# Two shifted-window attention layers on one core: statistics by pairs of images, two-part output projection, a separate order for the last images, and unread products on TensorE

## The chip, the cores and the metric

The kernel runs on one core of one Trainium2 chip. The metric is the device time of the whole program in microseconds (us); lower is better. The kernel before ran twice, at 763.71 and 770.17 us, so its median is 766.94 us. A further, profiled execution took 770.32 us.

## The reference, cut to what matters

The input is 32 images of 16 x 16 tokens with 256 channels, in float32. The same block is applied twice, each time with its own weights:

```
x = x + attention_0(group_norm(x))
x = x + attention_1(group_norm(x))

group_norm(v): 32 groups of 8 channels; mean and variance over the 256 tokens and the 8 channels
attention(x):
    xs = roll(x, (-4, -4)), cut into 4 windows of 8 x 8 = 64 tokens
    q, k = xw @ Wq.T, xw @ Wk.T;  v = xw @ Wv.T + bv       16 heads of 16 channels
    qn, kn = q / max(|q|, 1e-12), k / max(|k|, 1e-12)
    logits = qn @ kn.T * exp(min(logit_scale, log 100)) + 16 * sigmoid(bias table) (-inf across the shift's seams)
    o = softmax(logits) @ v
    z = o @ Wo.T + bo, windows put back, roll(z, (4, 4))
```

The bias table comes from a small two-layer network over 225 relative positions and is the same for all images of a layer. Nothing links one image to another, but an image's second layer needs its first.

## The kernel before, in words

**Jobs and rounds.** A job is one image in one layer; there are 64 (32 images, then the same 32 in layer 1). All x stays on the chip as `x_all`, with channels on the partitions. The work is a hand-written software pipeline. In round j every engine runs its `iteration(j, ...)`, which touches four jobs: `now` = j, `before` = j-1, `older` = j-2, `oldest` = j-3. Ahead of them come the group statistics of job j+3 (WARM = 3), the group roots of job j+2 and the normalised input of job j+1. Rounds -3 to 66 are run (`run`, L211 to L225). Most are bodies of hardware loops of two rounds each, in which semaphore counts and image addresses are computed in registers: on TensorE rounds 4 to 61, on the other engines rounds 4 to 27 and 36 to 59 (SyncE's first loop ends at 25). The rest are written out with constants. No scheduler moves anything: each engine runs its instructions in the written order, and semaphores alone tie the engines together.

**What TensorE does in a round** (`iteration`, L512 to L537): `sum_groups` of job j+2 (L433, one product that averages the statistics over groups); `project_qk` of `now` (L380, two halves of six products of 512 columns, into the two banks of `ps_qk`); `turn_back` of `oldest` (L392, four transposes of the attention output into `ps_mix`); `turn` of `before` (L404, eight transposes of q and k); `project_out` of `oldest` (L414 and L419: eight products with the rounded part `mixed_hi`, then four with the rest, into the same bank `z_cols` of `ps_mix`, with one signal `z_done` after all twelve); `score` of `before` (L469, 32 row-tiled products of 32 rows by 64 columns); `mix` of `older` (L486, one product of 64 rows and 128 columns, then L496, 63 products of 64 x 64, into `ps_mix`); `project_v` of `now` (L508, twelve products, into the second bank of `ps_qk`). An fp32 product is two instructions in the trace, so 32 products are 64 there.

**What waits for what.** `mix` overwrites the bank that `project_out` filled, so its first product (L486) waits until VectorE has added both halves of the residual (`add_residual`, L794, signal `x_updated`); that waits for `z_done`. `project_v` waits for `unit_ready`: ScalarE squares q and k (L574), VectorE sums (L758), ScalarE takes a logarithm and an exponential as seed (L609, L618), GpSimd does a Newton step (L943 to L953), VectorE scales (L783). ScalarE turns scores into `probs` by `exp`, in two instructions of 1024 columns (L643); GpSimd multiplies them by `exp_bias` in four (L963). VectorE divides (`divide`, L816 to L823) after `mix` and so gives `o_rows` to `turn_back` one round later.

**Start and end.** Layer 0's `exp_bias` is made from the bias table, which goes out to memory and comes back spread over the partitions (`keep_table`, `spread_bias`); four VectorE multiplications (L737) in round 0 finish it. SyncE issues x loads six jobs ahead, each when the last but one has landed. After round 63 the rounds simply run on with ever fewer jobs; all of them use the same `ps_mix`, so each `mix` waits for the residual before it. A flag, computed from the least softmax sum, decides at the end whether the whole is repeated in a slower exact form; on this input it is not.

## Time and profile before

| | us |
|---|---|
| two runs | 770.17, 763.71 (median 766.94) |
| profiled execution | 770.32 |
| its span, first to last instruction | 768.5 |
| TensorE busy | 728.5 (95%) |
| GpSimd busy | 553.6 (72%) |
| VectorE busy | 503.5 (66%) |
| ScalarE busy | 498.5 (65%) |

The span is the time from the first to the last instruction of the one profiled execution; 1.8 us of its 770.32 lie around it. A busy TensorE is not TensorE at its peak: matmuls are pipelined, and the end of one is modelled. "PEld" is its weight load, which overlaps the products. A gap of TensorE is read best from the end of a weight load to the start of the next. Its clock is granted at one of two levels, 2.4 GHz (shown as 1.00) or 1.2 GHz (0.50); a window in between has both.

### The profile page before, as it was taken

The numbers are of one execution on the slowest core, as the hardware profiler recorded it, in microseconds if no ns is written. First come the engines' busy times: TensorE is split into PE (matmuls) and PEld (weight loads), VectorE is DVE, ScalarE is ACT, GpSimd is POOL, SyncE is SP. The second block draws the span as 40 slices with busy tenths as digits, with TensorE's granted clock in tenths as the row PEclk, the third lists the DMA queues.
The fourth block names the chain that finished last, engine by engine and source line by source line (L and its number), as shares of the span: only waits on it lengthen the run. The fifth ranks groups of instructions, "written<-read, shape, count | busy, mean of one in ns | idle before, by whom it ended". The sixth has DMA issues, their size and how long they took to land.

```text
span 768.5 us, 38488 instructions
## 1 busy us (share of the span) xinstructions
PE 728.5 (95%) x15518; PEld 652.5 (85%) x15518; DVE 503.5 (66%) x1177; ACT 498.5 (65%) x848; POOL 553.6 (72%) x913
## 2 busy tenths in 40 slices
PE   3689899999999999999999999999999999999995
PEld 3578788888888889898989888888888888888984
DVE  4545466666666666667777667677766767776642
ACT  4556467676677667676777676666667666666650
POOL 4475668777877787788888777877777787777660
PEclk9789899999999999999999999999999999999995
DMA  4666200000000000000000000000000000000000
GB/s 116 156 157 172 65 0 0 0 1 0 0 0 0 0 0 0 0 0 0 1 0 0 28 28 14 27 27 25 16 27 27 14 27 27 27 14 27 29 31 32
DMA packets 14041, 21.45 MB, mean 28 GB/s; under 512 B 3756, under 2 KB 5045, under 8 KB 14005
## 3 DMA queue, kind: packets, MB, share of 16 engines
q1 hardware_dynamic: 13461, 20.23, 8.8%
q10 hardware_dynamic: 544, 0.79, 0.3%
q8 instruction: 17, 0.28, 0.2%
q14 instruction: 19, 0.16, 0.1%
HBM read 12.60 MB, written 8.42 MB: 27 GB/s over the span
## 4 chain that ended last, share of the span: by engine, by line
PE 89%; issue 3%; DVE 3%; DMA 2%; DVEq 1%; ACT 0%; SPq 0%; ACTq 0%
PE ps_qk L380 24%; PE ps_mix L496 17%; PE ps_qk L508 14%; PE ps_mix L414 9%; PE ps_score L404 7%; PE ps_score L469 6%; PE ps_mix L419 4%; PE ps_mix L392 4%; PE ps_mix L486 3%; DVE x_out L794 2%; DMA bias_rev<-table_scratch 1%; PE ps_score L433 1%; DMA table_scratch<-table 1%; DMA cpb<-in_L_cpb 0%; DVE exp_bias L737 0%
## 5 line engine op out<-in xcount | busy, mean ns | idle before, releaser
L963 POOL TENSOR_TENSOR probs<-probs,exp_bias 128x512 f32<-128x512 f32 x256 | 326.0, 1305 | 18.9 <-ACT probs L643 18.9
L380 PE MATMUL ps_qk<-w_qk,xn 128*128 128x512 f32 x768 | 200.0, 410 | 0.0
L643 ACT ACTIVATE probs<-ps_score,lower 128x1024 f32<-128x1024 f32 x128 | 135.7, 1111 | 66.8 <-PE ps_score L469 66.8
L380 PEld LDWEIGHTS ps_qk<-w_qk,xn 128*128 128x128 f32 x768 | 144.0, 194 | 30.2
L496 PE MATMUL ps_mix<-v_ones,probs 64*64 64x17 f32 x8064 | 133.4, 209 | 3.4 <-issue 3.4
L574 ACT ACTIVATE squares<-ps_qk 128x512 f32<-128x512 f32 x128 | 77.0, 602 | 87.1 <-PE ps_qk L380 87.1
L758 DVE TENSOR_REDUCE sums_sq<-squares 128x32 f32<-128x512 f32 x128 | 87.2, 682 | 68.9 <-ACT squares L574 68.8
L496 PEld LDWEIGHTS ps_mix<-v_ones,probs 64*64 64x64 f32 x8064 | 126.8, 136 | 5.5 <-issue 3.7
L783 DVE SCALAR_TENSOR_TENSOR unit<-root,ps_qk 128x512 f32<-128x512 f32 x128 | 82.4, 683 | 58.9 <-POOL root L953 58.9
L508 PE MATMUL ps_qk<-w_v,xn 128*128 128x256 f32 x768 | 113.9, 300 | 5.4 <-DVE unit L783 4.6
L508 PEld LDWEIGHTS ps_qk<-w_v,xn 128*128 128x128 f32 x768 | 100.2, 198 | 7.7 <-issue 6.0
L943 POOL TENSOR_TENSOR refined<-sums_sq,seed 128x66 f32<-128x66 f32 (+2 forms) x66 | 21.3, 322 | 97.6 <-ACT seed L618 97.5
L651 ACT ACTIVATE v_ones<-ps_qk 128x512 f32<-128x512 f32 x64 | 38.4, 601 | 77.4 <-PE ps_qk L508 77.4
L919 POOL TENSOR_TENSOR xn<-xn 128x512 fp32r<-128x512 f32 x64 | 82.0, 1281 | 5.5 <-ACT xn L581 5.5
L596 ACT ACTIVATE q_own<-ps_score,own_head 128x512 f32<-128x512 f32 x128 | 81.1, 693 | 0.0
L414 PE MATMUL ps_mix<-mixed,w_o 128*128 128x256 f32 x512 | 78.5, 296 | 1.4 <-ACT mixed L588 1.4
L469 PE MATMUL ps_score<-q_own,k_rows 32*64 32x128 f32 x4096 | 77.2, 278 | 2.4 <-DVE k_rows L767 1.2
L414 PEld LDWEIGHTS ps_mix<-mixed,w_o 128*128 128x128 f32 x512 | 65.0, 190 | 9.1 <-ACT mixed L588 2.0
L626 ACT ACTIVATE xn<-x_all,g_off,root 128x256 f32 (+1 forms) x128 | 69.5, 596 | 3.3 <-POOL g_off L956 3.3
L469 PEld LDWEIGHTS ps_score<-q_own,k_rows 32*64 32x64 f32 x4096 | 61.8, 130 | 11.2 <-ACT q_own L596 2.8
L404 PE MATMUL ps_score<-ident,unit 128*128 128x128 f32 x512 | 66.3, 273 | 0.0
L404 PEld LDWEIGHTS ps_score<-ident,unit 128*128 128x128 f32 x512 | 58.0, 140 | 0.3
(73 smaller groups left out, 867.8 us busy)
## 6 DMA issues: line engine op xcount, KB each, us to landing
x_all<-in_x SPq DMA_DIRECT2D x32, 256.0 KB, 3.1
out<-x_out SPq DMA_DIRECT2D x32, 256.0 KB, 2.1
bias_rev<-table_scratch SPq DMA_DIRECT2D x4, 452.0 KB
w_qk_in<-in_L_matrices ACTq DMA_DIRECT2D x1, 512.0 KB, 4.6
w_o_in<-in_L_matrices SPq DMA_DIRECT2D x4, 128.0 KB
w_qk_in<-in_L_matrices SPq DMA_DIRECT2D x1, 512.0 KB, 5.5
w_v_in<-in_L_matrices ACTq DMA_DIRECT2D x1, 256.0 KB, 4.9
w_v_in<-in_L_matrices SPq DMA_DIRECT2D x1, 256.0 KB, 6.2
```

The costliest lines, as they stand in the source:

```text
L380: last = nc.tensor.matmul(ps_qk[:, e, :], xn[:, px, t.parity, c, e * P:(e + 1) * P], w_qk[:, pw, c, :], start=(c == 0 and i == 0), stop=(c ...
L404: last = nc.tensor.transpose(to[:, e, c, :], unit[:, e, (n * CC + c) * P:(n * CC + c + 1) * P], ident[:, :])
L414: nc.tensor.matmul(z_cols[:, c, :], w_o[:, part, a, c * P:(c + 1) * P], mixed[:, 0, a, :], start=(c + a + part == 0), stop=False, skip_gro ...
L469: last = nc.tensor.matmul(ps_score[w * N:(w + 1) * N, r, cols:cols + 2 * N], k_rows[at, e, c, w * N:(w + 1) * N], q_own[at, e, c, w, :, :] ...
L496: last = nc.tensor.matmul(mix_cols[a * N:(a + 1) * N, w, (e * CC + c) * GROUPS + r, :], probs[at, t.parity, r, e, c, a, :], v_ones[at, t.p ...
L508: last = nc.tensor.matmul(v_cols[:, e, :], xn[:, px, t.parity, c, e * P:(e + 1) * P], w_v[:, pw, c, :], start=(c == 0 and i == 0), stop=(c ...
L596: nc.scalar.activation(q_own[:, :, :, :, a, :].rearrange("p e c w n -> p (e c w) n"), q_turned_to.rearrange("p e c (w n) -> p (e c w) n", ...
L643: nc.scalar.activation(probs[:, t.parity, 2 * i:2 * i + 2, :, :, :, :].rearrange("p r e c a n -> p r (e c a n)"), ps_score[:, 2 * i:2 * i ...
L758: nc.vector.tensor_reduce(sums_sq[:, e * NORMS:(e + 1) * NORMS], squares[:, e, :].rearrange("p (h d) -> p h d", d=HD), AX_X, ALU.add).then ...
L783: nc.vector.scalar_tensor_tensor(out=unit[:, e, :].rearrange("p (h d) -> p h d", d=HD), in0=by, scalar=INV_NORM_TOP, in1=ps_qk[:, e, :].re ...
L919: nc.gpsimd.tensor_tensor(xn[:, 1, t.parity, :, :], xn32[:, :, :], xn[:, 0, t.parity, :, :], ALU.subtract).then_inc(xn_ready, 1)
L963: nc.gpsimd.tensor_tensor(pr, pr, exp_bias[:, t.layer, r, :, :, :, :].rearrange("p e c a n -> p (e c a n)"), ALU.mult).then_inc(weighted, 1)
```

## The change

It rewrites the rounds, the start and the end together.

- **Statistics by pairs.** `sum_groups`, `group_variance` and the group part of the root chain run in even rounds only, for jobs j+2 and j+3 together (four columns instead of two). The moments are taken four jobs ahead (AHEAD = 4). The last variance step gets a tensor of fours in place of a constant.
- **TensorE's round.** `turn_back` of `oldest` goes between the halves of `project_qk`. `project_out` finishes channel half 0 (four products with the rounded part, two with the rest), signals, then half 1, and signals again. `mix` begins with one tiny product of 32 rows, 64 columns and one output column that carries its waits, and then has all 64 products in 64 x 64 form; its waits for `v_ready` and `mixed_ready` are gone.
- **The others' rounds.** ScalarE rounds `mixed` ahead of `xn` and takes `exp` in four instructions of 512 columns. VectorE forms `mixed`'s rest between the two sums of squares, and each half of the residual waits for its own signal.
- **Start.** Both first images are loaded first; the bias tables of the two layers are made apart (layer 1's in rounds 0 and 1); layer 0's `exp_bias` is multiplied by GpSimd in round 1; the sum of output biases moves from round 1 to 2; TensorE gets unread products (`keep_busy`: 7, 3, 9 and 12). SyncE holds the x loads from round 4 on until `unit_ready` has counted six jobs.
- **End.** After round 63 a `drain` of its own follows. The last three jobs use three different places for `mix`, `turn_back` and `project_out`: `ps_mix`, `ps_qk` and `ps_score`. The last job's weighting is shared between GpSimd and VectorE, its `mix` is split in halves around `turn_back` of the job before, and its output is stored in two halves. Three unread products stand ahead of the last `turn_back` and five behind it. Eight tiny memsets on GpSimd (into `unread`) stand in round 60.

```
+AHEAD = 4
...
-        def both_passes(engine, iteration, loops=((4, 28), (IMAGES + 4, 60))):
+            half, parity = divmod(JOBS - 1 + JOBS * exact, 2)
+            drain(Job(half, parity, None, exact))
...
+        def pair(j, base):
+            return job(j, base, 2) if j % 2 == 0 else None
+        def home_of(t, last):
+            return (ps_mix, ps_qk, ps_score)[last]
+        def back_of(t, last):
+            return home_of(t, last)[:, 1, :].rearrange("p (a t) -> p a t", a=2)
+        def kept_of(t, last):
+            return xn[:, :, 0, :, :] if last == 2 else mixed
...
SyncE
+                if j == 4 and not base.exact:
+                    sp.wait_ge(unit_ready, 2 * 6)
                 if j >= 0:
                     load_x(job(j, base, PREFETCH))
...
TensorE, project_out
+                for c in range(CC):
                     for a in range(2):
                         for part in range(2):
-                                             start=(c + a + part == 0), stop=False, skip_group_check=True)
-                pe.wait_ge(mixed_ready, t.count(1, 1))
-                for c in range(CC):
+                            nc.tensor.matmul(home[:, c, 0:TOKENS], w_o[:, part, a, c * P:(c + 1) * P], kept[:, 0, a, :],
+                                             start=(a + part == 0), stop=False, skip_group_check=True)
+                    if c == 0:
+                        pe.wait_ge(mixed_ready, t.count(1, 1))
                     for a in range(2):
+                        done = nc.tensor.matmul(home[:, c, 0:TOKENS], w_o[:, 0, a, c * P:(c + 1) * P], kept[:, 1, a, :],
                                                 start=False, stop=(a == 1), skip_group_check=True)
-                last.then_inc(z_done, 1)
+                    done.then_inc(z_done, 1)
TensorE, mix
-                past(pe, x_updated, t.count(2, 0))
-                past(pe, mixed_ready, t.count(1, 0))
-                pe.wait_ge(v_ready, t.count(1, 1))
-                pe.wait_ge(weighted, t.count(4, 4))
-                nc.tensor.matmul(mix_cols[:, 0, 0, :], probs[0:N, t.parity, 0, 0, 0, :, :]...
+                if last == 0:
+                    past(pe, x_updated, t.count(2, 0))
+                    pe.wait_ge(weighted, t.count(4, 4 - 2 * t.exact))
+                    nc.tensor.matmul(ps_mix[0:N, 0, 511:512], ident[0:32, 0:N], ident[0:32, 0:1], start=True, stop=True, skip_group_check=True)
...
TensorE, iteration
+                if j != 0:
+                    sum_groups(j, base)
+                if j == -1 and not base.exact:
+                    keep_busy(9)
                 project_qk(now, 0)
+                turn_back(oldest)
                 project_qk(now, 1)
-                turn_back(oldest)
+                if j == 0:
+                    sum_groups(j, base)
+                    if not base.exact:
+                        begin_table(1)
+                        keep_busy(12)
+                        end_table(1)
                 turn(before)
                 project_out(oldest)
+                if j == 2 and not base.exact:
+                    sum_out_bias()
-                score(j, base, before)
+                score(before)
...
+            def drain(base):
+                now, before, older = (job(JOBS - 1, base, -k) for k in range(3))
+                turn(now)
+                turn_back(older)
+                score(now)
+                project_out(older)
+                mix(before, 1)
+                mix(now, 2, (0,))
+                turn_back(before, 1)
+                mix(now, 2, (1,))
+                project_out(before, 1)
+                if not base.exact:
+                    keep_busy(3)
+                turn_back(now, 2)
+                if not base.exact:
+                    sum_lost()
+                    keep_busy(5)
+                project_out(now, 2)
+            def keep_busy(n):
+                ones = v_ones[:, 0, :, :, :, :, :].rearrange("p e c r a d -> p (e c r a d)")[:, 0:P]
+                for _ in range(n):
+                    nc.tensor.matmul(ps_score[:, 3, 0:P], ones, ones, start=True, stop=True, skip_group_check=True)
...
ScalarE, iteration
                 square(now, 0)
+                keep_mixed(oldest)
                 round_xn(job(j, base, 1))
                 square(now, 1)
-                keep_mixed(oldest)
...
-                for i in range(GROUPS // 2):
-                    exp(before, i)
+                for r in range(GROUPS):
+                    exp(before, r)
...
VectorE, add_residual and drain
+                dve.wait_ge(z_done, t.count(2, c + 1))
...
+                keep_k(now)
+                keep_rest(older)
+                for r in (1, 3):
+                    dve.wait_ge(exped, now.count(4, r + 1))
+                    multiply_probs(nc.vector, now, r, last_weighted)
+                divide(before, 1)
+                for c in range(CC):
+                    add_residual(older, c)
+                keep_rest(before, 1)
+                divide(now, 2)
...
+                for c in range(CC):
+                    add_residual(before, c, 1)
+                keep_rest(now, 2)
...
+                for c in range(CC):
+                    add_residual(now, c, 2)
...
GpSimd, iteration
+                if j == 1 and not base.exact:
+                    for e in range(2):
+                        for c in range(CC):
+                            multiply_bias(nc.gpsimd, 0, e, c)
...
+                if j == JOBS - 4:
+                    for k in range(8):
+                        nc.gpsimd.memset(unread[:, k:k + 1], 0.0).then_inc(moment_step, 1)
```

TensorE, round 3 (the first round with every step, written out), before:

```order
L433 MATMUL ps_score<-bn_sum,consts 128x4
L380 MATMUL ps_qk<-w_qk,xn 128x512 x12
L392 MATMUL ps_mix<-ident,o_rows 128x2x64 x4
L404 MATMUL ps_score<-ident,unit 128x128 x8
L414 MATMUL ps_mix<-mixed,w_o 128x256 x8
L419 MATMUL ps_mix<-mixed,w_o 128x256 x4
L469 MATMUL ps_score<-q_own,k_rows 64x128 x32
L486 MATMUL ps_mix<-v_ones,probs 128x17
L496 MATMUL ps_mix<-v_ones,probs 64x17 x63
L508 MATMUL ps_qk<-w_v,xn 128x256 x12
```

The same round in the changed kernel:

```order
L450 MATMUL ps_qk<-w_qk,xn 128x512 x6
L463 MATMUL ps_mix<-ident,o_rows 128x2x64 x4
L450 MATMUL ps_qk<-w_qk,xn 128x512 x6
L475 MATMUL ps_score<-ident,unit 128x128 x8
L487 MATMUL ps_mix<-mixed,w_o 128x256 x4
L492 MATMUL ps_mix<-mixed,w_o 128x256 x2
L487 MATMUL ps_mix<-mixed,w_o 128x256 x4
L492 MATMUL ps_mix<-mixed,w_o 128x256 x2
L544 MATMUL ps_score<-q_own,k_rows 64x128 x32
L561 MATMUL ps_mix<-ident 64x1
L577 MATMUL ps_mix<-v_ones,probs 64x17 x64
L590 MATMUL ps_qk<-w_v,xn 128x256 x12
```

The group product is gone from this odd round, the transposes stand inside the projection, the first channel half of the output is signalled six products earlier, and the 128-column product at the head of `mix` has become one of 64 columns by one.

TensorE, the end of the program, before (from the last `score` on):

```order
L469 MATMUL ps_score<-q_own,k_rows 64x128 x32
L486 MATMUL ps_mix<-v_ones,probs 128x17
L496 MATMUL ps_mix<-v_ones,probs 64x17 x63
L392 MATMUL ps_mix<-ident,o_rows 128x2x64 x4
L414 MATMUL ps_mix<-mixed,w_o 128x256 x8
L419 MATMUL ps_mix<-mixed,w_o 128x256 x4
L486 MATMUL ps_mix<-v_ones,probs 128x17
L496 MATMUL ps_mix<-v_ones,probs 64x17 x63
L541 MATMUL ps_score<-consts,lost 1x1
L392 MATMUL ps_mix<-ident,o_rows 128x2x64 x4
L414 MATMUL ps_mix<-mixed,w_o 128x256 x8
L419 MATMUL ps_mix<-mixed,w_o 128x256 x4
```

And now, from the `mix` of the last job but one:

```order
L577 MATMUL ps_qk<-v_ones,probs 64x17 x64
L577 MATMUL ps_score<-v_ones,probs 64x17 x32
L463 MATMUL ps_qk<-ident,o_rows 128x2x64 x4
L577 MATMUL ps_score<-v_ones,probs 64x17 x32
L487 MATMUL ps_qk<-mixed,w_o 128x256 x4
L492 MATMUL ps_qk<-mixed,w_o 128x256 x2
L487 MATMUL ps_qk<-mixed,w_o 128x256 x4
L492 MATMUL ps_qk<-mixed,w_o 128x256 x2
L656 MATMUL ps_score<-v_ones 128x128 x3
L463 MATMUL ps_score<-ident,o_rows 128x2x64 x4
L660 MATMUL ps_mix<-consts,lost 1x1
L656 MATMUL ps_score<-v_ones 128x128 x5
```

The last two jobs' `mix` stand next to each other, in other banks; the last job's twelve output products follow behind the rows shown.

GpSimd in round 1 of the changed kernel:

```order
L1085 TENSOR_TENSOR xn<-xn 128x512
L1109 TENSOR_TENSOR refined<-sums_sq,seed 128x64
L1111 TENSOR_TENSOR refined<-refined,seed 128x64
L1113 TENSOR_TENSOR refined<-threes,refined 128x64
L1119 TENSOR_TENSOR root<-refined,seed 128x64
L276 TENSOR_TENSOR exp_bias<-bias_rev,masks 128x4x128 x4
L282 TENSOR_TENSOR probs<-probs,exp_bias 128x512 x4
```

The row L276 is new here: the four bias products stood on VectorE in round 0 before (L737).

## Rows read from the trace of the kernel before

**Rows 1.** The page: engines' busy time, granted clock in 40 slices, chain of waits.

```profile
PE 728.5 (95%) x15518; PEld 652.5 (85%) x15518; DVE 503.5 (66%) x1177; ACT 498.5 (65%) x848; POOL 553.6 (72%) x913
...
PEclk9789899999999999999999999999999999999995
```

**Rows 2.** Stretches: start:end, length, busy of PE, PEld, DVE, ACT, POOL; PEclk, DMA, GB/s.

```profile
107.98:729.73 621.75, 615.69 (x13548) 552.61 (x13549) 433.42 (x1007) 429.93 (x729) 479.70 (x775) 1.00 0.03 12
...
704.28:715.20 10.92, 10.92 (x243) 9.87 (x242) 6.78 (x16) 7.65 (x13) 7.74 (x11) 1.00 0.06 24
715.20:725.90 10.70, 10.70 (x245) 9.65 (x240) 6.00 (x12) 7.64 (x13) 7.82 (x11) 1.00 0.07 25
...
749.60:768.50 18.90, 10.46 (x158) 9.28 (x158) 4.80 (x13) 0.60 (x2) 1.19 (x1) 0.53 0.09 33
```

**Rows 3.** Groups by line, 107.98 to 729.73 us: busy, mean ns | idle before.

```profile
L486 PEld LDWEIGHTS ps_mix<-v_ones,probs 64*128 64x128 f32 x112 | 16.5, 185 | 18.9 <-issue 18.7 <-DVE x_out L794 0.2
```

**Rows 4.** Timeline of a layer-1 round in the loops: start, length, engine, line, idle before.

```profile
512.19 0.63 PE L419 MATMUL ps_mix<-mixed,w_o 128*128 128x256 f32 x4
...
512.75 0.96 PEld L469 LDWEIGHTS ps_score<-q_own,k_rows 32*64 32x64 f32 x64
512.75 1.21 PE L469 MATMUL ps_score<-q_own,k_rows 32*64 32x128 f32 x64
...
513.09 0.88 DVE L794 SCALAR_TENSOR_TENSOR x_out<-ps_mix,out_bias,x_all 128x256 f32<-128x256 f32 x2 [0.57 <-PE ps_mix L419]
...
514.09 0.29 PEld L486 LDWEIGHTS ps_mix<-v_ones,probs 64*128 64x128 f32 x2 [0.37 <-issue]
...
514.41 1.95 PEld L496 LDWEIGHTS ps_mix<-v_ones,probs 64*64 64x64 f32 x126
514.75 1.28 DVE L783 SCALAR_TENSOR_TENSOR unit<-root,ps_qk 128x512 f32<-128x512 f32 x2 [0.79 <-POOL root L953]
...
516.39 1.48 PEld L508 LDWEIGHTS ps_qk<-w_v,xn 128*128 128x128 f32 x12
...
517.13 0.69 DVE L823 TENSOR_TENSOR o_rows<-ps_mix,inv_sums 128x512 f32<-128x512 f32 x1
...
518.05 1.18 PE L380 MATMUL ps_qk<-w_qk,xn 128*128 128x512 f32 x4
```

**Rows 5.** Timeline of round 63, all engines written out, no group product.

```profile
735.47 0.96 PEld L469 LDWEIGHTS ps_score<-q_own,k_rows 32*64 32x64 f32 x64
735.47 1.21 PE L469 MATMUL ps_score<-q_own,k_rows 32*64 32x128 f32 x64
735.58 0.88 DVE L794 SCALAR_TENSOR_TENSOR x_out<-ps_mix,out_bias,x_all 128x256 f32<-128x256 f32 x2 [0.34 <-PE ps_mix L419]
...
736.60 0.29 PEld L486 LDWEIGHTS ps_mix<-v_ones,probs 64*128 64x128 f32 x2 [0.17 <-DVE x_out L794]
```

**Rows 6.** Timeline of the start.

```profile
12.17 1.29 POOL L919 TENSOR_TENSOR xn<-xn 128x512 fp32r<-128x512 f32 x1 [1.78 <-ACT xn L581]
...
16.94 4.53 PE L380 MATMUL ps_qk<-w_qk,xn 128*128 128x512 f32 x12
...
27.56 3.98 DVE L737 TENSOR_TENSOR exp_bias<-bias_rev,masks 128x512 f32<-128x512 f32 x4 [1.05 <-DMA bias_rev<-table_scratch]
...
37.33 4.98 POOL L963 TENSOR_TENSOR probs<-probs,exp_bias 128x512 f32<-128x512 f32 x4 [0.29 <-ACT probs L643]
...
78.73 2.63 PEld L508 LDWEIGHTS ps_qk<-w_v,xn 128*128 128x128 f32 x12
```

**Rows 7.** Timeline of the end, after round 63.

```profile
740.43 0.62 PE L392 MATMUL ps_mix<-ident,o_rows 128*128 128x128 f32 x4
...
744.85 2.05 PE L496 MATMUL ps_mix<-v_ones,probs 64*64 64x17 f32 x126
...
753.31 3.60 PE L496 MATMUL ps_mix<-v_ones,probs 64*64 64x17 f32 x126
...
763.50 0.88 DVE L794 SCALAR_TENSOR_TENSOR x_out<-ps_mix,out_bias,x_all 128x256 f32<-128x256 f32 x2 [2.30 <-PE ps_mix L419]
```

462 lines of the change are left out of this document (271 added, 191 removed).

## Prediction

> **What bounds the kernel now.** I read the page first. TensorE is busy for 728.5 of 768.5 us, no other engine for more than 553.6 [rows 1], so the kernel is a chain of TensorE work. Next I cut the span by the clock row of the page and by stretches. From round 7's first projection (107.98) to round 63's (729.73), 56 rounds pass in 621.75 us at clock 1.00 [rows 2]: 11.10 us a round. Ahead of that lie 107.98 us for seven rounds and a start, behind it 38.8 us. So there are three places: the steady rounds (81% of the span), the start, the end.
>
> In a steady round TensorE is never idle for long; the groups by line show where it is. Ahead of L486, the first product of `mix`, it stood idle for 18.9 us in these 56 rounds, 0.34 us each [rows 3]. The row says "issue", so I went to the timeline: in layer 1 the loads of `score` end at 513.71, the second residual on VectorE at 513.97, L486 starts at 514.09 [rows 4]. In round 63, where registers need not be computed, they end at 736.43 and 736.46, and L486 starts at 736.60 [rows 5]. The start keeps 0.12 to 0.14 us behind the residual while the gap itself changes from 0.38 to 0.17. The gap is VectorE's residual, and VectorE began it late because `z_done` comes once, after all twelve products, and register work adds 0.27 us to it in the loop (512.82 to 513.09) [rows 4].
>
> **The steady rounds.** Four edits touch TensorE's time.
> 1. Group product every second round. The round from 704.28 has one (10.92 us), the next has none (10.70) [rows 2]. It costs 0.22, so half, 0.11, goes per round. This is sure.
> 2. The gap. Half 0 of the residual now starts when the first six products are done, under the other six and the transposed k; only half 1 is left behind the last product. From 512.82 with the same 0.27 us of register work and half of the 0.88 us it ends at 513.53, before the loads of `score` end at 513.71 [rows 4]. What remains is the change of step. Lower bound: 0.03 us, from the end of L486's loads (514.38) to L496's start (514.41) [rows 4], a change of form without a wait. Upper bound: the 0.17 of round 63 [rows 5]. I take 0.12, nearer the upper end, since two waits stand in this step and none in the other. Against the mean of 0.34 [rows 3] that saves 0.22, between 0.17 and 0.30.
> 3. The first product. L486 takes 514.09 to 514.41, 0.32 us [rows 4]. In its place come a 32 x 64 product with one column (two instructions) and one more 64 x 64 product (two). The 126 instructions of L496 load in 1.95 us, 15.5 ns each, and the 64 of L469 in 0.96, 15 ns each [rows 4]: four of these are 0.06 us. With a change of form (0.04 to 0.07) I take 0.13, so 0.19 saved. Bounds: nothing saved, or 0.26.
> 4. `turn_back` inside the projection and the split `project_out` issue the same instructions; on TensorE I cost them at nothing. Their cover is that `o_rows` is ready at 517.82 and the projection begins at 518.05 [rows 4]; the transposes now come six products (1.4 us) after that, so VectorE may be 1.6 us late before TensorE feels it.
>
> Sum: 0.11 + 0.22 + 0.19 = 0.52 us a round, low 0.28, high 0.67. Over 57 rounds (7 to 63) this is 29.6 us, from 16 to 38. I take 28, because something is late next: `project_v` needs the first unit, ready at 515.39, and starts at 516.39 [rows 4]. That is 1.0 us of slack, of which edits 2 and 3 use 0.4. ScalarE squares the second half later by the transposes (0.62 us in the end's row [rows 7]), but `mixed`, which stood behind these squares, now stands ahead of them, so the logarithm moves by little. Four `exp` in place of two cost ScalarE two more instructions; it is busy 429.93 of 621.75 us [rows 2] and nothing on TensorE waits for the last of them within the round. GpSimd's 479.70 us [rows 2] gain nothing new but the eight memsets, well under 1 us once.
>
> **The start.** Job 0's input is complete on GpSimd at 13.46 (12.17 + 1.29), but the first projection starts at 16.94 [rows 6]: TensorE's group product for job 2 stood ahead of it. It is moved behind, so 3.4 us go. Then 91.0 us pass for rounds 0 to 6, against 7 x 11.10 = 77.7: 13.3 us of waits, half clock and pauses in TensorE's stream. Half clock shows in L508's twelve loads, 2.63 us at 78.73 [rows 6] against 1.48 in the steady round [rows 4]. The 31 unread products of the start and the held x loads work against both, and the sum of output biases leaves the path of round 1. Against this, GpSimd gets four bias products in round 1. No row has them on GpSimd. VectorE took 3.98 us for the four, and GpSimd 4.98 for four contiguous products of the same size [rows 6]; I take 5, and twice that as the upper bound. They stand ahead of job 0's weighting and of round 2's Newton step and I count 4 of the 5 us on the path in round 2. Of the 13.3 us I count 10 as won back, since round 0 waits for its own chain with nothing else to do in either kernel. Balance: 3.4 + 10 - 4 = 9 us gained. Bounds: 3.4 + 0 - 5, so about 2 lost (the whole bias price on the path and none of the 13.3 back), and 3.4 + 13.3 = 17 gained.
>
> **The end.** From 740.43 to the last residual's end (763.50 + 0.88 = 764.38) it takes 23.95 us [rows 7], and three times `mix`, transposes, projection and residual follow each other in one bank, with the clock at 0.53 after 749.6 [rows 2]. L496 then takes 3.60 us instead of 2.05 [rows 7]. I laid the new order out by hand from these lengths at full clock, in us after 740.43: turn 0.9, turn back 1.4, `score` 2.1 to 3.3 (it waits for q on ScalarE), `exp` to 5.7, the first `project_out` to 4.9, `mix` of the last but one to 7.0, GpSimd and VectorE end weighting at 6.6, first half of the last `mix` 8.0, second 9.9, divided 11.8, turned back 12.3, `mixed` 13.1 and its rest 13.9, the projection's halves 14.1 and 14.9, last residual 15.4. That saves 8.5. Half clock in the last projections could give back 1 to 3 us; the unread products (as long as a transpose each, a quarter of the 0.62 us of four [rows 7]) stand where TensorE waits for VectorE anyway. I take 8, from 5 to 10. The last store is of half the size, which I count at nothing.
>
> **Sum.** 28 + 9 + 8 = 45 us. Against the profiled execution's own 770.32 us (span 768.5 and 1.8 around it) that is 725.3. The median of the two runs lies 3.4 us below the profiled execution, so I put the forecast between the two, at **724 us**. All low ends together give 770 - 19 = 751, all high ends 705; together they are unlikely.
>
> **Rivals.**
> - *The change of form rules the gap.* What if L486 waits for the array to empty, as its start 0.13 us after the modelled end of L469's last product (513.96) would allow [rows 4]? Then splitting `z_done` gains nothing, edits 2 and 3 save only what the shorter product does (0.15), and a round gains 0.26: 15 us instead of 28, so **737 us**. Against it: with the same forms the gap is 0.17 in round 63, and L486 starts there before that modelled end (735.47 + 1.21 = 736.68) [rows 5]. Chance 0.08. The Trainium skill, TensorEngine Tiling (Array Packing), Key Properties, says that changing the tiling mode drains TensorE. By that rule the pause stays and the time would be the 737 us above; the trace bounds the pause of a change of form at the 0.17 us of round 63, and so speaks for a small one.
> - *The unit chain becomes the bound.* Later squares and longer ScalarE work use up the 1.0 us of slack, and the round stays at 10.9. Against it: ScalarE's work ahead of the logarithm is the same in sum, and VectorE's too. It gives 56 x 0.2 = 11 us in place of 28: **741 us**. Chance 0.07.
> - *Slower: `turn_back` stalls the projection.* It now stands in front of the second half, whose squares feed the sums, the Newton step, the units, and at last `divide`, which feeds `turn_back`. If `o_rows` comes more than 1.6 us later than in rows 4, each round waits in mid-projection and the delay feeds itself, since VectorE is in order. From 2.1 us late a round is longer than 11.10; at 2.7 us the rounds lose 34 us, and the whole stands at **787 us**. Against it: VectorE is busy 433.42 of 621.75 us [rows 2]. Chance 0.02.
> - *The start fails.* GpSimd's bias products are twice as long as their nearest row and the clock does not hold: the start loses 2 to 5 instead of gaining 9, which gives **737 us**. Chance 0.08, inside the range. On the price, the Trainium skill, GPSIMD Engine Reference, Engine selection, has two-input elementwise work about twice as slow on GpSimd as on VectorE. By that page the four would take twice the 3.98 us of VectorE, an estimate of 8 us, and the time would be some 3 us above my sum.
>
>
> **Chances and range.** Forecast 0.75, the others as above. A measurement of this kernel can tell about 2%, 15 us, from no change: 751.6 us and below is faster. All rivals but the slower one are faster still; I keep 0.05 for within 2% (several low ends at once) and 0.03 for slower, 0.92 for faster. The range that leaves out 2 in 10 reaches from 709 (start and rounds near their high ends) to 740.
>
> **What would show it.** Idle ahead of the first `mix` product near 0.1 us; round time 10.6 us in both layers, with the difference between layers gone; first projection near 13.5 us; no gap ahead of `turn_back` inside the projection; round 7 at some 96 us; the last residual 16 us after the last `project_v`. I would be wrong if `project_v` or the second projection half showed a new wait, if the gap stayed at 0.3 us, or if GpSimd's bias products took over 2 us each.

## The result, and the profile after

The changed kernel takes **713.38 us** (two runs, 713.31 and 713.44) against 766.94 of the kernel before: a ratio of 0.930, with a 95% interval of 0.913 to 0.947. Run again, four times beside seven runs of before (median 769.83), it took 713.49, ratio 0.9263 (0.9217 to 0.9309). The forecast was 724 with a range of 709 to 740. So the sign, the mechanism and the range held; the sum was 11 us short. Its three terms missed by 15 us (the rounds, more gained), 1 us (the start, more) and 5 us (the end, less), so that the end's miss covered a part of the rounds'. One of all executions of the kernel before took 2373.71 us, for a reason that no profile shows, and is left out of the ratios. The profiled execution took 713.44 us, of which 711.6 are the span: 56.9 less than the 768.5 before.

Page of the changed kernel: busy time by engine, the granted clock in 40 slices, the shares of the chain of waits.

```profile
PE 690.4 (97%) x15658; PEld 632.6 (89%) x15658; DVE 468.6 (66%) x1049; ACT 518.6 (73%) x976; POOL 551.2 (77%) x888
...
PEclk8979999999999999999999999999999999999998
...
PE 92%; POOL 3%; DVE 2%; issue 2%; DMA 1%; ACT 1%; SPq 0%; POOLq 0%; DVEq 0%; ACTq 0%
```

Beside [rows 1], TensorE is busy 38 us less in all, and its idle time went from 40 us to 21: some was work that is gone, some was waiting. Where, the stretches tell. First the 56 rounds from round 7's first projection to round 63's, then round 63.

```profile
97.87:677.09 579.22, 578.22 (x13611) 530.57 (x13610) 400.08 (x894) 447.80 (x842) 474.19 (x753) 1.00 0.06 19
677.09:687.35 10.26, 10.26 (x244) 9.44 (x243) 5.94 (x12) 6.46 (x12) 6.42 (x10) 1.00 0.07 26
```

Against [rows 2] the account of the 56.9 us is:

| stretch | before | after | gained | forecast |
|---|---|---|---|---|
| up to round 7 | 107.98 | 97.87 | 10.1 | 9 |
| 56 rounds, 7 to 62 | 621.75 | 579.22 | 42.5 | 27.5 |
| round 63 | 10.70 | 10.26 | 0.4 | 0.5 |
| to the last residual's end | 23.95 | 20.69 | 3.3 | 8 |
| from there to the span's end | 4.12 | 3.56 | 0.6 | 0 |

(The timeline of before has round 7's first product at 107.84, where [rows 2] has 107.98: 0.1 us between the first two rows of the table.)

Of the signs that the prediction named, the round time came out at 10.34 us and not 10.6, and alike in both layers (two rounds took 20.64 us from 97.87 on in layer 0 and 20.61 from 408.90 on in layer 1); the idle time ahead of the first `mix` product is 0 and not 0.1; the first projection started at 15.70 and not near 13.5; round 7 at 97.87 and not 96.

A round fell from 11.10 to 10.34 us, 0.76, where the sum had 0.52 and, rounded down, gave 0.49. The timeline of one round of layer 1, with the group product of the next round at its end (start, length, engine, line; elsewhere brackets say how long the engine had been idle, and for whom; "issue" there is idle time for which the profile shows no wait). One fp32 product is two loads, so the 64 products of `mix` are 128 loads here:

```profile
408.79 1.23 PEld L450 LDWEIGHTS ps_qk<-w_qk,xn 128*128 128x128 f32 x6
...
410.06 0.59 PEld L463 LDWEIGHTS ps_mix<-ident,o_rows 128*128 128x128 f32 x4
...
410.62 1.24 PEld L450 LDWEIGHTS ps_qk<-w_qk,xn 128*128 128x128 f32 x6
...
411.90 1.03 PEld L475 LDWEIGHTS ps_score<-ident,unit 128*128 128x128 f32 x8
...
412.90 0.54 PEld L487 LDWEIGHTS ps_mix<-mixed,w_o 128*128 128x128 f32 x4
...
414.17 1.02 DVE L929 SCALAR_TENSOR_TENSOR x_out<-ps_mix,out_bias,x_all 128x256 f32<-128x256 f32 x2
414.44 0.35 ACT L739 ACTIVATE seed<-logs,consts 128x64 f32<-128x64 f32 x1
414.48 0.96 PEld L544 LDWEIGHTS ps_score<-q_own,k_rows 32*64 32x64 f32 x64
...
415.43 0.19 PEld L561 LDWEIGHTS ps_mix<-ident 32*64 32x64 f32 x2
...
415.63 1.96 PEld L577 LDWEIGHTS ps_mix<-v_ones,probs 64*64 64x64 f32 x128
...
417.61 1.46 PEld L590 LDWEIGHTS ps_qk<-w_v,xn 128*128 128x128 f32 x12
...
419.00 0.30 PEld L508 LDWEIGHTS ps_score<-bn_sum,consts 128*128 128x128 f32 x2
...
419.22 1.25 PEld L450 LDWEIGHTS ps_qk<-w_qk,xn 128*128 128x128 f32 x6
```

Three things to see, each against [rows 4]. The two residuals (L929) end at 415.19, the loads of `score` (L544) at 415.44, and the head of `mix` (L561, its first small product) starts at 415.43: no pause at all, where 0.34 stood in the mean [rows 3]. From the head to the first of the 128 loads it is 0.20 us, where L486 took 0.32. And the twelve products of the projection with the transposes between them take 1.27 + 0.56 + 1.28 = 3.11 us, where the same sixteen instructions took 2.67 + 0.56 = 3.23 in round 62 of before. The group product still costs its 0.22 (419.00 to 419.22), in every second round.

### The profile page after: what moved, and what is told of

Same layout as the page of the kernel before. It is cut to its first block, busy times and chain, and to the rows that moved or that the text cites. A ratio compares the mean times of both kernels' runs of the same rounds, so it can differ in the third digit from the quotient of the medians.

```text
span 711.6 us, 38739 instructions
## 1 busy us (share of the span) xinstructions
PE 690.4 (97%) x15658; PEld 632.6 (89%) x15658; DVE 468.6 (66%) x1049; ACT 518.6 (73%) x976; POOL 551.2 (77%) x888
## 4 chain that ended last, share of the span: by engine, by line
PE 92%; POOL 3%; DVE 2%; issue 2%; DMA 1%; ACT 1%; SPq 0%; POOLq 0%; DVEq 0%; ACTq 0%
PE ps_qk L450 25%; PE ps_mix L577 17%; PE ps_qk L590 14%; PE ps_score L544 9%; PE ps_mix L487 8%; PE ps_score L475 7%; PE ps_mix L492 4%; PE ps_mix L463 4%; PE ps_score L656 1%; POOL probs L282 1%; DMA x_all<-in_x 1%; POOL exp_bias L276 1%; PE ps_score L508 1%; DVE probs L282 0%; PE ps_score L577 0%
## 5 line engine op out<-in xcount | busy, mean ns | idle before, releaser
L450 PE MATMUL ps_qk<-w_qk,xn 128*128 128x512 f32 x768 | 209.4, 409 | 0.2
L764 ACT ACTIVATE probs<-ps_score,lower 128x512 f32<-128x512 f32 x256 | 155.2, 689 | 56.2 <-PE ps_score L544 56.1
L450 PEld LDWEIGHTS ps_qk<-w_qk,xn 128*128 128x128 f32 x768 | 136.6, 191 | 24.3 <-DVE unit L919 0.2
L577 PE MATMUL ps_mix<-v_ones,probs 64*64 64x17 f32 x7936 | 129.1, 208 | 2.0 <-issue 2.0
L577 PEld LDWEIGHTS ps_mix<-v_ones,probs 64*64 64x64 f32 x7936 | 122.7, 136 | 5.1 <-issue 2.2
L590 PE MATMUL ps_qk<-w_v,xn 128*128 128x256 f32 x768 | 109.2, 293 | 5.4 <-DVE unit L919 5.4
L590 PEld LDWEIGHTS ps_qk<-w_v,xn 128*128 128x128 f32 x768 | 96.2, 194 | 7.5 <-DVE unit L919 4.2
L1109 POOL TENSOR_TENSOR refined<-sums_sq,seed 128x64 f32<-128x64 f32 (+1 forms) x65 | 22.0, 338 | 82.1 <-ACT seed L739 82.1
L487 PE MATMUL ps_mix<-mixed,w_o 128*128 128x256 f32 x496 | 82.4, 288 | 0.0
L544 PE MATMUL ps_score<-q_own,k_rows 32*64 32x128 f32 x4096 | 77.2, 278 | 1.6 <-ACT q_own L717 1.5
L544 PEld LDWEIGHTS ps_score<-q_own,k_rows 32*64 32x64 f32 x4096 | 61.7, 130 | 9.8 <-ACT q_own L717 2.0
L487 PEld LDWEIGHTS ps_mix<-mixed,w_o 128*128 128x128 f32 x496 | 66.2, 189 | 0.2 <-issue 0.2
```

What stands on the lines that cost most here:

```text
L450: last = nc.tensor.matmul(ps_qk[:, e, :], xn[:, px, t.parity, c, e * P:(e + 1) * P], w_qk[:, pw, c, :], start=(c == 0 and i == 0), stop=(c ...
L487: nc.tensor.matmul(home[:, c, 0:TOKENS], w_o[:, part, a, c * P:(c + 1) * P], kept[:, 0, a, :], start=(a + part == 0), stop=False, skip_gro ...
L544: last = nc.tensor.matmul(ps_score[w * N:(w + 1) * N, r, cols:cols + 2 * N], k_rows[at, e, c, w * N:(w + 1) * N], q_own[at, e, c, w, :, :] ...
L577: done = nc.tensor.matmul(mix_cols[a * N:(a + 1) * N, w, (e * CC + c) * GROUPS + r, :], probs[at, t.parity, r, e, c, a, :], v_ones[at, t.p ...
L590: last = nc.tensor.matmul(v_cols[:, e, :], xn[:, px, t.parity, c, e * P:(e + 1) * P], w_v[:, pw, c, :], start=(c == 0 and i == 0), stop=(c ...
L764: nc.scalar.activation(probs[:, t.parity, r, :, :, :, :].rearrange("p e c a n -> p (e c a n)"), ps_score[:, r, :], ACT.Exp, bias=lower[:, ...
```

## The experiments

All ran beside the kernel before. The changed kernel itself ran only in the first of three such sets, and the medians of before were 769.83, 769.69 and 770.86 us in them, so a difference of about a microsecond to the changed kernel says nothing. The differences below are between medians (to 713.49 where nothing else is said), and where a stretch is given it is from the profiled execution: round 7's first projection to round 63's, 579.22 us in the changed kernel (579.25 in its second profile) and 621.75 in the kernel before.

**again**: the changed kernel, unedited.

> The changed kernel once more, on the chip and in the job of the three that follow, so that each of them is read against it. Every theory expects the 713 us of its first runs, within 2 us, and some 0.93 of the kernel before.

713.49 us (710.34 to 714.77). Its profile has the same 56 rounds to 0.03 us, while the ends of two profiles of one kernel differ by 1 us. So the rounds can be read to a few hundredths, the start and the end only to about one microsecond.

**one_signal**: the residual waits for both halves again.

```diff
-                dve.wait_ge(z_done, t.count(2, c + 1))
+                dve.wait_ge(z_done, t.count(2, c + 1 if last else 2))
```

> In the rounds both halves of the residual wait for the second signal of the output projection again; everything else is the changed kernel. Theory A (the pause ahead of mix was the late residual): the residual ends 0.4 us later, the pause comes back at 0.25 to 0.45 us in each of 57 loop rounds, 14 to 25 us more, so 727 to 738. Theory B (the pause was the change of the tiling form): nothing changes, 713 within 1 us.

729.49 us, 16.0 more; the 56 rounds took 595.14, 15.9 more: 0.28 a round. Timeline rows of two rounds:

```profile
519.69 0.19 PEld L561 LDWEIGHTS ps_mix<-ident 32*64 32x64 f32 x2 [0.32 <-DVE x_out L929]
...
530.27 0.19 PEld L561 LDWEIGHTS ps_mix<-ident 32*64 32x64 f32 x2 [0.37 <-issue]
```

The pause is back ahead of the head; one of the two rows puts it down to the residual, the other to nothing that the profile shows. Theory A holds, near its lower end; nothing else was edited, so the late signal is the cause. The forecast had given this edit 0.22.

**wide_head**: the old 64 x 128 product heads `mix` again, for the ident product and one of the 64.

```diff
-                    nc.tensor.matmul(ps_mix[0:N, 0, 511:512], ident[0:32, 0:N], ident[0:32, 0:1], start=True, stop=True, skip_group_check=True)
+                    nc.tensor.matmul(mix_cols[:, 0, 0, :], probs[0:N, t.parity, 0, 0, 0, :, :].rearrange("p a n -> p (a n)"),
+                                     v_ones[0:N, t.parity, 0, 0, 0, 0, :], start=True, stop=True, skip_group_check=True)
...
                                 for w in range(2):
+                                    if last == 0 and e + c + r + a + w == 0:
+                                        continue
```

> Mix begins with the old product of 64 rows and 128 columns in place of the 32 x 64 one with one column; both signals of the output projection stay. Theory A: the head costs 0.13 us more a round by the two traces (0.33 against 0.20 us), and as its form is not that of score, the pause of a change of form stands ahead of it, 0.1 us at most: 7 to 13 us more, 720 to 726. Theory B (the form rules the pause): the whole 0.34 us come back with it and the head's 0.13, 27 us more, 740.

733.39 us, 19.9 more; the rounds 595.99, 16.8 more: 0.30 a round (in this profile round 7 also starts 4.7 us later). Two rows of one round:

```profile
523.79 0.96 PEld L544 LDWEIGHTS ps_score<-q_own,k_rows 32*64 32x64 f32 x64
524.92 0.29 PEld L561 LDWEIGHTS ps_mix<-v_ones,probs 64*128 64x128 f32 x2 [0.17 <-issue]
525.25 1.95 PEld L580 LDWEIGHTS ps_mix<-v_ones,probs 64*64 64x64 f32 x126
```

The residual is early here, and yet 0.17 us pass ahead of the head, in each round (8.9 us in 52). The head itself takes 0.33. So two costs belonged to the old head: 0.13 of length, which the forecast had (0.19), and 0.17 of a pause that the residual had covered. The sum of both is the 0.30 of a round. Theory A had the length and at most 0.1 of pause, 13 us at most; theory B had 27. The measured 16.8 lies between them.

**turn_back_behind**: both halves of the projection first, `turn_back` behind them; ScalarE's and VectorE's order follow.

```diff
                 project_qk(now, 0)
-                turn_back(oldest)
                 project_qk(now, 1)
+                turn_back(oldest)
...
                 square(now, 0)
-                keep_mixed(oldest)
                 round_xn(job(j, base, 1))
                 square(now, 1)
+                keep_mixed(oldest)
...
                 sum_norms(base, now, 0)
-                keep_rest(oldest)
                 sum_norms(base, now, 1)
+                keep_rest(oldest)
```

> turn_back stands behind both halves of the projection again, and ScalarE's and VectorE's steps that follow it are back in their old places. Theory C (its new place shortens the projection): the trace gives the twelve products of the projection 2.55 us of loads against 2.67 before, so the round gets 0.1 us longer, 6 to 8 us in all, 719 to 721. Theory D (the place costs and gives nothing, the shorter loads come from elsewhere): 713 within 1.5 us.

741.64 us, 28.2 more, 0.52 a round (608.23): both theories were far off. The timeline names it:

```profile
516.50 0.53 PEld L487 LDWEIGHTS ps_mix<-mixed,w_o 128*128 128x128 f32 x4
517.33 0.30 PEld L492 LDWEIGHTS ps_mix<-mixed,w_o 128*128 128x128 f32 x2 [0.29 <-DVE mixed L911]
...
528.33 0.30 PEld L492 LDWEIGHTS ps_mix<-mixed,w_o 128*128 128x128 f32 x2 [0.29 <-DVE mixed L911]
```

`project_out` by halves wants the rest of `mixed` after four products; the old order wanted it after eight. With the transposes late, VectorE has it ready 0.29 us after the loads of those four (15.2 us in 51 rounds, by the groups). The loads of two such groups overlap by 0.07 where nothing waits, so the wait costs more than the 0.29: from start to start 0.83 us (516.50 to 517.33) in place of 0.47 (412.90 to 413.37 in the changed kernel), 0.36. Another 0.12 is the projection, twelve products in one piece again, and 0.04 lies between the transposes of q and k and the output products (1.04 in place of 1.00 us). That is the 0.52. So the place of `turn_back`, with ScalarE's and VectorE's steps that follow it, is what makes the early signal possible; the three were not moved one by one.

The next four ask about the two ends.

**no_busy_end**: the eight unread products of the end are left out.

```diff
                 project_out(before, 1)
-                if not base.exact:
-                    keep_busy(3)
                 turn_back(now, 2)
                 if not base.exact:
                     sum_lost()
-                    keep_busy(5)
                 project_out(now, 2)
```

> The changed kernel without the eight unread products at the end (three ahead of the last but one transposes, five ahead of the last projection). Theory E1 (they fill the array where it would stand idle and so hold the clock): without them half clock covers more of the stretch after the last score, and the last residual ends 0.5 to 3 us later. Theory E2 (they only stand in the way: as now written, TensorE enters half clock at about 698 anyway, after a pause of 0.97 us that no product filled): nothing is lost, or up to 0.5 us is gained, and the granted clock of the last 15 us does not change. The whole stays within 0.5% of the changed kernel by both; the stretch from round 63's first projection to the last residual's end (30.95 us now) tells them apart.

713.80 us (712.01 to 715.36), no difference. From round 63's first projection to the last residual's end it takes 30.86 us, against 30.95 and 29.73 in the two profiles of the changed kernel. The granted clock from 690 on is 0.66 here, 0.81 and 0.80 there:

```profile
690.00:708.40 18.40, 16.25 (x366) 14.53 (x352) 10.49 (x22) 3.83 (x7) 3.15 (x3) 0.66 0.12 40
```

Without the products the last four groups of the projection stay at half clock (0.93 + 0.54 + 0.97 + 0.54 us of loads, against 0.54 + 0.30 + 0.54 + 0.30). But the three products also stand ahead of the last transposes, which are later by about as much. Not all of the lower clock is due to the edit: the first half of the last `mix`, which stands ahead of the place of the eight products, took 1.47 us here and 1.12 there. From that place on the granted clock is 0.50 here (703.08 to 708.40) and 0.76 in the changed kernel (702.04 to 708.04). So E1's mechanism can be seen, but its price cannot be told from the spread of this end, about a microsecond.

**gpsimd_weighs_end**: all four of the last job's products of probabilities on GpSimd.

```diff
-                for r in (1, 3):
-                    dve.wait_ge(exped, now.count(4, r + 1))
-                    multiply_probs(nc.vector, now, r, last_weighted)
...
-                for r in (0, 2):
+                for r in range(GROUPS):
                     weigh(now, r)
```

> The last job's four products of probabilities all on GpSimd instead of two there and two on VectorE. Theory F1 (the two engines slow each other: in the changed kernel two on each took 2.97 us, about 1.48 each, on both engines at once): alone, GpSimd takes about 1.35 us each as in the steady round, 5.4 us for the four, so the first product of the last mix starts some 2.4 us later than now (697.4 against 695.0), and the whole is 2 to 2.5 us longer. Theory F2 (1.48 us is what a product of this form takes on either engine, with no contention): four take 5.9 us and the mix starts 2.9 us later. Theory F3 (contention was most of it): each takes under 1.0 us alone and nothing is lost.

714.89 us (713.38 to 715.95), 1.4 more, which is hardly clear of the noise; the pause ahead of the last `mix` is 2.2 us in place of 0.9. Alone, GpSimd takes 4.95 us for the four, 1.24 each and not F1's 1.35, and the `mix` starts 1.4 us later, not 2.4. Of the three theories F1 is the nearest: the changed kernel's 1.48 each is the two engines' slowing of each other.

**bias_on_vector**: layer 0's four `exp_bias` products on VectorE in round 0, as before.

```diff
                 if j == 0:
                     moments(ahead)
+                if j == 0 and not base.exact:
+                    for e in range(2):
+                        for c in range(CC):
+                            mask_bias(0, e, c)
...
-                if j == 1 and not base.exact:
-                    pool.wait_ge(masks_in, 2 * 16)
-                    pool.wait_ge(bias_in, 2 * 16)
-                    for e in range(2):
-                        for c in range(CC):
-                            multiply_bias(nc.gpsimd, 0, e, c)
```

> Layer 0's four exp_bias products back on VectorE, in round 0, instead of on GpSimd in round 1. Theory G1 (my start term: the 6.0 us on GpSimd delay job 0's weighting and with it rounds 2 and 3): round 4 starts 2 to 4 us earlier than 62.91, the whole is 2 to 4 us shorter. Theory G2 (VectorE's units are as much on the path in rounds 1 and 2, and its 4 us delay them): round 4 starts within 1 us of now, or up to 4 us later.

714.30 us (710.05 to 717.65): the same. Round 2 starts at 41.12 in place of 37.50, round 3 at 52.45 in place of 52.34, round 4 at 62.76 in place of 62.91. On VectorE the four take 3.82 us and push job 1's unit; on GpSimd they take 6.00 and push job 0's weighting; a round later it is the same. This is G2.

This run's profile shows something that was not asked for. Its last stretch, with the same program there, ran at full clock throughout:

```profile
690.00:704.30 14.30, 12.88 (x374) 11.82 (x358) 10.26 (x22) 3.68 (x7) 3.00 (x3) 1.00 0.12 41
```

From the end of round 63 (687.62) to the last residual's end (704.29) it takes 16.7 us, against 20.7 in the first profile of the changed kernel. Up to the second half of the last `mix` the two are alike to 0.01 us. Then the changed kernel has a pause of 0.97 us in mid-`mix` and half clock behind it: together they cost this end 4 us, the pause 1 and the half clock 3.

**no_busy_start**: the 31 unread products of the start are left out.

```diff
                     pe.wait_ge(filled, FILLS)
-                    keep_busy(7)
...
-                if j == -1 and not base.exact:
-                    keep_busy(9)
...
-                        keep_busy(12)
...
-                    keep_busy(3)
```

> The changed kernel without the 31 unread products of the start (7, 9, 12 and 3). Theory H1 (they hold the clock over the waits of rounds 0 to 3): more half clock up to 50 us and round 4 starts 2 to 6 us later than 62.91. Theory H2 (the waits of the start are for other engines, so that TensorE's clock hardly matters): round 4 starts within 1 us of now, and the whole is the same.

717.36 us (714.72 to 720.84), 3.9 more. Round 4 starts at 67.44, 4.5 later, round 7 at 100.76, 2.9 later: H1. The first projection starts where it did (15.76, its loads at 15.73) but at half clock:

```profile
15.73 4.11 PEld L450 LDWEIGHTS ps_qk<-w_qk,xn 128*128 128x128 f32 x12 [4.34 <-issue]
```

In the changed kernel the same twelve loads take 2.63 us (15.67 to 18.30).

**double_head**: the new head twice.

```diff
                     nc.tensor.matmul(ps_mix[0:N, 0, 511:512], ident[0:32, 0:N], ident[0:32, 0:1], start=True, stop=True, skip_group_check=True)
+                    nc.tensor.matmul(ps_mix[0:N, 0, 511:512], ident[0:32, 0:N], ident[0:32, 0:1], start=True, stop=True, skip_group_check=True)
```

> The changed kernel with the 32 x 64 product with one column that heads each mix issued twice. In the changed kernel the head takes 0.19 to 0.20 us from its load to the first load of the 128 products. Theory J1 (the head's own cost is two loads of some 15 ns each, and the rest of the 0.2 is the array changing form behind it): the second one costs 0.03 to 0.05 us a round, 2 to 3 us in all. Theory J2 (the head itself costs 0.19): 57 x 0.19 = 11 us more.

719.48 us (717.68 to 722.89), 6.0 more; the rounds took 585.68, 6.4 more or 0.115 each. Neither theory: the second costs over twice J1's figure and six tenths of J2's.

```profile
522.48 0.19 PEld L561 LDWEIGHTS ps_mix<-ident 32*64 32x64 f32 x2
522.59 0.19 PEld L562 LDWEIGHTS ps_mix<-ident 32*64 32x64 f32 x2
522.79 1.96 PEld L578 LDWEIGHTS ps_mix<-v_ones,probs 64*64 64x64 f32 x128
```

From one head to the next it is 0.11, from the second to the 64 x 64 products 0.20. So 0.11 of the head is its own, and the other 0.09 I put down to the step to the next form. No run begins `mix` with a 64 x 64 product straight behind `score`; whether the small product is worth its 0.11 against that is open.

**head_on_before**: the kernel before, with only the new head.

```diff
-                nc.tensor.matmul(mix_cols[:, 0, 0, :], probs[0:N, t.parity, 0, 0, 0, :, :].rearrange("p a n -> p (a n)"),
-                                 v_ones[0:N, t.parity, 0, 0, 0, 0, :], start=True, stop=True, skip_group_check=True)
+                nc.tensor.matmul(ps_mix[0:N, 0, 511:512], ident[0:32, 0:N], ident[0:32, 0:1], start=True, stop=True, skip_group_check=True)
...
-                                    if e + c + r + a + w == 0:
-                                        continue
```

> The kernel before with nothing but the new head: the 32 x 64 product in the place of the 64 x 128 one, all 128 products in the loop. The end of mix's predecessor, VectorE's residual, stays as late as it was. Theory K1 (the two costs of the head add up: 0.13 us of a shorter head, and 0.1 to 0.17 us of a pause that belongs to the change of form and goes with it, though it lies partly under the residual): 0.13 to 0.30 a round, 7 to 17 us less than before. Theory K2 (the residual holds the head, whatever it is): 0.13 x 57 = 7 us less, and the pause ahead of the head stays at 0.34.

765.30 us (761.39 to 768.46), ratio 0.9932 (0.9907 to 0.9958): by the ratio 5.2 us less than before, between 3.2 and 7.2. Its 56 rounds took 617.21 us, 4.5 less, with one pause of 1.20 us in them that the profile puts down to nothing, so some 0.10 a round. K2's 7 lies inside, K1's upper part does not. The group row of 120 to 670 us (busy, mean ns | idle before) shows why: the pause is still 17.2 us in 50 rounds, 0.34 each.

```profile
L486 PEld LDWEIGHTS ps_mix<-ident 32*64 32x64 f32 x100 | 9.3, 129 | 17.2 <-issue 16.6
```

**split_on_before**: the kernel before, with only the split of `project_out`.

```diff
-        z_cols = ps_mix[:, 0, :].rearrange("p (c t) -> p c t", c=CC)
+        z_cols = ps_mix[:, :, 0:TOKENS]
...
-                                             start=(c + a + part == 0), stop=False, skip_group_check=True)
-                pe.wait_ge(mixed_ready, t.count(1, 1))
-                for c in range(CC):
+                                             start=(a + part == 0), stop=False, skip_group_check=True)
+                    if c == 0:
+                        pe.wait_ge(mixed_ready, t.count(1, 1))
...
-                last.then_inc(z_done, 1)
+                    last.then_inc(z_done, 1)
...
-                if c == 0:
-                    dve.wait_ge(z_done, t.count(1, 1))
+                dve.wait_ge(z_done, t.count(2, c + 1))
```

> The kernel before with nothing but the split of project_out: its products by output half, one bank for each, and a signal and a residual for each half; turn_back stays ahead of turn. Theory L1 (the signal alone does it): the residual ends 0.4 us earlier, the pause ahead of mix falls from 0.34 to about 0.17, 57 x 0.17 = 10 us less. Theory L2 (it needs turn_back's new place: with four instead of eight products ahead of it, the wait for the rest of mixed is uncovered by some 0.3 us in each round, as it was in the changed kernel with turn_back behind the projection): the gain is used up, from 3 us less to 8 us more than before, with a pause of some 0.3 us ahead of the first two products with the rest of mixed.

780.91 us (777.37 to 781.46), ratio 1.0138 (1.0096 to 1.018): 10 us **slower** than before. The pause falls as L1 says, to 0.17 (8.4 us in 49 rounds), and L2's wait comes in its place, 0.28 us, with a round of 11.30; the loss is somewhat above L2's upper end of 8.

```profile
518.17 0.54 PEld L414 LDWEIGHTS ps_mix<-mixed,w_o 128*128 128x128 f32 x4
518.99 0.30 PEld L419 LDWEIGHTS ps_mix<-mixed,w_o 128*128 128x128 f32 x2 [0.28 <-DVE mixed L775]
519.22 0.55 PEld L414 LDWEIGHTS ps_mix<-mixed,w_o 128*128 128x128 f32 x4
519.70 0.31 PEld L419 LDWEIGHTS ps_mix<-mixed,w_o 128*128 128x128 f32 x2
...
521.28 0.29 PEld L486 LDWEIGHTS ps_mix<-v_ones,probs 64*128 64x128 f32 x2 [0.17 <-issue]
```

The 56 rounds took 633.06, 0.20 more each. The wait costs more than the 0.28 of idle time: from start to start the two groups lie 0.82 us apart (518.17 to 518.99), and 0.48 in the other half of the same round (519.22 to 519.70), where nothing waits. So the wait costs 0.34, the shorter pause gives back 0.17, and 0.17 of the 0.20 is accounted for.

**vector_weighs_end**: all four of the last job's products on VectorE.

```diff
-                for r in (1, 3):
+                for r in range(GROUPS):
                     dve.wait_ge(exped, now.count(4, r + 1))
                     multiply_probs(nc.vector, now, r, last_weighted)
...
-                for r in (0, 2):
+                for r in ():
                     weigh(now, r)
```

> The last job's four products of probabilities all on VectorE, none on GpSimd. GpSimd alone took 1.24 us for one (4.95 for four), and both engines at once 1.48 each. Theory M1 (VectorE alone takes about 0.7 us, as for other products of 128 x 512, and only the two at once are slow): the four follow the four exps (0.6 us each) and end about 1 us earlier than now, TensorE's pause ahead of the last mix goes, the last residual ends 1 us earlier, and 3 us more where the clock then holds. Theory M2 (VectorE takes 1.0 to 1.2 alone): they end at the same time or 1 us later than now.

714.63 us (711.99 to 716.43). M1's first half is right: alone each takes 0.69 us, the last `mix` starts 4.6 us after the last `score` in place of 5.7, and the pause ahead of it is gone. The microsecond isn't in the total: the second half of that `mix` stood still for 0.89 us for nothing that the profile shows, the clock fell (its first 29 loads took 19 ns each, the last 35 took 33), and from the last `score` to the last residual's end it took 17.9 us, where the changed kernel took 18.7 and, at full clock, bias_on_vector 14.7. VectorE's own four products, minimum, median and maximum in ns:

```profile
L282 DVE TENSOR_TENSOR probs<-probs,exp_bias x4: 682/684/693, 693.1 to 694.9; 128x512 f32<-128x512 f32 x4
```

No variant beats the changed kernel by more than the spread of its runs.

## Why the prediction was right, and where it was short

**What bounds the kernel, and the sign.** Right. TensorE's own stream was the bound, and everything taken from it in a round came off the time. None of the rivals came true as it stood. GpSimd is busy 474 of 579 us and TensorE 578.

**Group product, 0.11 a round.** Right: 0.22 in every second round.

**The gap, 0.22 a round, and the first product, 0.19.** This is the step that was mis-sized. The four kernels with each of the two edits make a table; it is the idle time ahead of the head of `mix` in a round:

| | residual late | residual early |
|---|---|---|
| 64 x 128 head | 0.34 (before) | 0.17 (split_on_before, wide_head) |
| 32 x 64 head | 0.34 (head_on_before), 0.26 (one_signal, 13.7 us in 52 rounds) | 0.00 (the changed kernel) |

The forecast left 0.12 of pause for a change of form in the changed kernel, whatever the head. It did not ask which change of form. The old head has another form than `score`, and 0.17 stand ahead of it even when nothing else is late; round 63 had shown the same 0.17 [rows 5], and there it was put down to the residual. The new head has the form of `score` (32 x 64), and nothing stands ahead of it. So 0.34 went, not 0.22, and the head became shorter by 0.13, not 0.19: together 0.47 where the two terms had 0.41. What in the form counts, its rows, its columns or the operands that changed with it, no run tells apart. The Trainium skill, TensorEngine Tiling (Array Packing), Key Properties, says that a change of tiling mode drains TensorE. The trace agrees that such a change costs, with 0.17 us ahead of the old head, though no run shows that it is a drain; and the rival built on that rule failed because the change takes away that very change of form. The step from 32 x 64 to 64 x 64 that remains costs some 0.09 (double_head).

**`turn_back`'s place and the split `project_out`, costed at nothing.** Wrong in two ways. The projection by two sixes with four transposes between is 0.12 us shorter, 6.7 us over 56 rounds, and no row of before could have given it; turn_back_behind shows that it belongs to the place. And the place is a condition for the early signal: the forecast read 513.53 for the residual's end from the signal alone. It did not ask when the rest of `mixed` is ready if `project_out` wants it four products earlier. Without the new place that wait costs 0.36 a round, more than the 0.28 that the signal saves (one_signal), and on the kernel before the split alone is a loss of 10 us. In the change itself the two came together, so the error left no mark on the total: that was luck.

**The steady sum.** 0.11 + 0.34 + 0.13 + 0.12 = 0.70 of the 0.76 measured; the last 0.06 is spread over rows that differ by hundredths. That is 42.5 us in place of 28. The 28 had also been rounded down for a late `project_v`; no wait of its own showed there in the steady rounds.

**The start, 9 us.** Right in sum (10.1), wrong in its parts, so right by luck. The first projection moved from 16.94 to 15.70, 1.2 and not 3.4: the statistics of two images now stand on the way to the first root, and GpSimd completes job 0's input at 15.56, not at 13.46 as the forecast assumed.

```profile
10.28 1.03 POOL L1109 TENSOR_TENSOR refined<-sums_sq,seed 128x4 f32<-128x4 f32 x1 [2.21 <-ACT seed L739]
...
14.29 1.27 POOL L1085 TENSOR_TENSOR xn<-xn 128x512 fp32r<-128x512 f32 x1 [0.96 <-ACT xn L701]
```

Rounds 0 to 6 gained 8.9 where 10 less 4 stood. But seven rounds of the new length are 72.4 us, 5.3 less than seven of the old, which the term had left out; what lies above them fell only from 13.3 us to 9.8 (82.2 less 72.4). So 3.5 of waits and half clock were won back, where the sum had 6. The unread products are worth 3 to 4 us there (no_busy_start); what the held x loads and the tables' new places did, no run isolates. And GpSimd's bias products took 6.00 us, not 5:

```profile
33.80 6.00 POOL L276 TENSOR_TENSOR exp_bias<-bias_rev,masks 128x512 f32<-128x512 f32 x4
```

They cost the whole no more than VectorE's 3.82 would have (bias_on_vector).

**The end, 8 us.** This term was mis-sized too: 3.3 in the first profile and some 4.5 in the second, so below the range of 5 to 10. The order laid out by hand took 15.4 us at full clock; where the clock stayed full it took 16.7 (bias_on_vector), 7.3 us less than before. The 1.3 between them is mostly one wait: both engines' products of the last job end at 694.87, not at some 0.7 each.

```profile
691.37 2.96 POOL L282 TENSOR_TENSOR probs<-probs,exp_bias 128x512 f32<-128x512 f32 x2 [1.65 <-ACT probs L764]
...
691.90 2.97 DVE L282 TENSOR_TENSOR probs<-probs,exp_bias 128x512 f32<-128x512 f32 x2 [1.38 <-ACT probs L764]
...
695.02 1.12 PE L577 MATMUL ps_score<-v_ones,probs 64*64 64x17 f32 x64 [0.88 <-DVE probs L282]
...
698.34 1.25 PE L577 MATMUL ps_score<-v_ones,probs 64*64 64x17 f32 x36 [0.97 <-issue]
...
700.97 1.05 PE L487 MATMUL ps_qk<-mixed,w_o 128*128 128x256 f32 x4
...
707.56 0.48 DVE L929 SCALAR_TENSOR_TENSOR x_out<-ps_score,out_bias,x_all 128x256 f32<-128x256 f32 x1 [0.22 <-PE ps_score L492]
```

The other 4 us are a pause and the half clock behind it. TensorE waited 0.88 us for VectorE, then stood 0.97 us in mid-`mix` with no wait in the program, and from there its products are at the lower of the two levels (L487 1.05 us for four instead of 0.62). The order laid out by hand had full clock throughout, the forecast gave half clock 1 to 3 us, and the term of 8 took off half a microsecond; the pause and the half clock together cost 4. What decides whether the clock falls at this place is open: in the profile of bias_on_vector a pause of 0.90 us ahead of the same `mix` was followed by no half clock at all, but there the pause in mid-`mix` did not come either; in the second profile of the changed kernel the clock fell right behind the pause of 0.96 us ahead of that `mix` (its first 64 loads took 1.55 us, not 1.05).

## What to carry to other kernels

Ahead of a small product that heads a stage, ask for each of its costs apart: who is late, whether its form (rows by columns) differs from its predecessor's, and its own length. The first two lie on top of each other in a trace, and only the kernel with both removed shows the gain (here 0.34 us a round, where either edit alone left at least 0.17). When a signal is split so that a consumer may start early, list what the reordered producer now wants earlier itself; here that wait alone cost 0.34 to 0.36 us a round, more than the early signal saved, and moving one group of transposes forward removed it.
